# Attention outputs kept transposed, divided per chunk of queries on GpSimd, in a fused attention and mixture-of-experts kernel

## The chip, the cores and the metric

The kernel runs on one core of one Trainium2 chip. The metric is device time in microseconds (us). Before the change the median of three runs is 1865.36 us (1862.76 to 1872.71). All durations and starts below come from one further, profiled execution.

## The reference

One pre-layer-norm transformer block on x of 2048 tokens by 512 features, in float32:

```
Q = norm(x) @ Wq + bq          # 32 heads of 16
K, V = norm(x) @ Wk + bk, norm(x) @ Wv + bv    # 8 heads of 16, each shared by 4 query heads
out = softmax(Q K^T / 4) V     # per head, all 2048 keys
x = x + out @ Wo + bo
logits = norm(x) @ gate_w.T    # 8 experts
w, idx = softmax over the two largest logits, their experts
x = x + sum of w * (norm(x) @ expert_w[idx].T + expert_b[idx])
```

## The kernel before

The engines run streams that were written by hand, each in program order, joined by semaphores. There are 16 token tiles of 128 (`NKT`), 4 chunks of 512 queries (`NC`), 8 groups of heads (`G`), each of 4 query heads with one key head (`REP`), and so 32 rounds (`N`), one for each group and chunk.

**Rounds.** Each round has 16 steps (`kt`, one key tile of 128). A step (`attention_step`) puts on TensorE two `max_unit` (L722: scores of a later round, 128 queries by 1024 keys, that VectorE reduces to maxima, L1040), four score units (L751: keys on the partitions, 512 queries on the columns), and the value products of the step two before (L761). ScalarE takes the exponential of each score unit (L591). The value product has 32 output rows for each head: 16 of the value and 16 equal rows with the sum of the exponentials, for 512 queries on the columns. So the outputs come out transposed, in bank 6, and ScalarE copies them to `o_acc` (L581).

**The ring of banks.** Score units go round three PSUM banks (`SBANKS`). The list `RING` holds the order of what takes a bank. Besides the 64 score units of a round it holds `outputs` (before score unit 16, step 4) and `maxima` (before score unit 44, step 11). `ring_bank_free` makes each entry wait for whatever used the entry three places before. Entry `outputs` is four transposes of `o_acc` (`output_transpose`, L775). VectorE divides them by the sums (`normalise`, L1064 and L1066) into `o_norm`, which is stored in `heads_out` with queries on the partitions. Entry `maxima` is one transpose of the 16 columns of maxima (L732). From it VectorE makes the two rows that shift the scores of the next round (`make_shift`, L1054 and L1057), right behind one more reduction (L1040) in its program.

**Output stage.** After the last round, for each of 16 token tiles, TensorE transposes the loaded heads (L866), ScalarE rounds them to the high part (L597) and VectorE makes the low part (L1112). TensorE multiplies with Wo, split in the same way, in 12 matmuls (L856). VectorE adds the residual (L1147, after GpSimd added the bias `bo` to it, L369) and takes mean and variance (L1153, L1150). The tiles of the chunk before are in the same loop: normalised on VectorE (L1120), transposed on TensorE (L873), copied by ScalarE to `xgT` (`gate_evac`, L608), multiplied with the gate weights (`gate_logits`, L883). The square root of the variance is taken once for each chunk of four tiles (L627). Four times 128 logits are copied (L613) and turned back (L893). The stage ends when VectorE gets the last of them (`gl_full`). In it the expert weights of four of eight experts are split (`expert_hi` L599, `expert_lo` L1107); the others come after it.

**After it.** A chain of small operations on VectorE chooses experts and slots, indirect DMAs of GpSimd scatter the tokens, 39 slots of 128 tokens go through the experts, and the results are gathered and summed. The change touches the last two stages only in where the splits of three or four experts stand.

Of the kernel before, what the change touches and what calls it, by code (L numbers as in the profile page):

```python
# [16 lines left out]
def preln_attention_moe(nc, x, Wq, bq, Wk, bk, Wv, bv, Wo, bo, gate_w, expert_w, expert_b, out):  # L17
# [39 lines left out]
    RING.insert(REP * 4, ("outputs", 0))  # L57
    RING.insert(REP * (MAX_T + 1) + 1, ("maxima", 0))
# [16 lines left out]
    heads_out = nc.dram_tensor("heads_out", [NC, P, TT, G + 1, REP * DK], F32).ap()  # L75
# [4 lines left out]
    with ExitStack() as ctx:  # L80
# [23 lines left out]
        mv = sb("mv", [P, TT, 2])  # L104
        std = sb("std", [P, TT])
# [10 lines left out]
        o_rec = sb("o_rec", [P, TT, REP, 1])  # L116
        o_norm = sb("o_norm", [P, TT, REP, DK])
# [16 lines left out]
        with nc.sbuf_tensor("we_raw", [P, E, KD, D], F32) as we_raw:  # L134
# [35 lines left out]
        EA = 4  # L170
        (_, xg, xgT, lgT, _, atT_hi, atT_lo, at), (we_hi, x2T_hi, x2T_lo) = in_turn(
            [("we_hi_early", [P, EA, KD, D], F32R),
             ("xg", [P, 2, D], F32), ("xgT", [P, 2, KD, P], F32),
             ("lgT", [E, CH], F32),
             ("spare", [P, 3 * D], F32),
             ("atT_hi", [P, 2, KD, P], F32R), ("atT_lo", [P, 2, KD, P], F32R),
             ("at", [P, 2, TT, D], F32)],
            [("we_hi", [P, E, KD, D], F32R), ("x2T_hi", [P, 2, KD, P], F32R), ("x2T_lo", [P, 2, KD, P], F32R)])

# [47 lines left out]
        oT_full = sem("oT_full")  # L227
        rec_ready = sem("rec_ready")
        onorm_ready = sem("onorm_ready")
        o_dma = sem("o_dma")  # L230
        at_dma = sem("at_dma")
        xr_dma = sem("xr_dma")
# [5 lines left out]
        at_full = sem("at_full")  # L238
        at_hi = sem("at_hi")
        at_evac = sem("at_evac")  # L240
        wo_full = sem("wo_full")
        x2_ready = sem("x2_ready")
        step_c = sem("step_c")
        mv2_ready = sem("mv2_ready")
# [42 lines left out]
        B_OUT, B_MAX = ring_bank(("outputs", 0)), ring_bank(("maxima", 0))  # L287
# [4 lines left out]
        def _(pool):  # L292
# [70 lines left out]
            pool.wait_ge(s_full, UNITS * N)  # L363
            for c in range(NC):
                pool.dma_start(x2_all[:, c * TT:(c + 1) * TT, :], x_t[:, c * TT:(c + 1) * TT, :]).then_inc(xr_dma, 16)
                pool.wait_ge(xr_dma, 16 * (c + 1))
# [22 lines left out]
        def _(sp):  # L389
# [49 lines left out]
            def store_heads(i):  # L439
                wait_first(onorm_ready, 1 + i + 1)  # L440
# [81 lines left out]
        def _(act):  # L522
# [92 lines left out]
            def chunk(c, with_gate, last):  # L615

                for t in range(TT):
                    if not (last and t == TT - 1):
                        attention_hi(TT * c + t + 1, t + 1)
# [679 lines left out]
```

## Time and profile before

| | us |
|---|---|
| median of 3 runs | 1865.36 |
| profiled execution, its own time | 1858.62 |
| its span | 1857.0 |
| first round begins | about 152 |
| `o_acc` of the last round copied (L581) | 1514.85 |
| last logits turned back (L893) | 1606.91 |
| first scatter (L375) | 1620.89 |
| last expert matmul ends, about | 1801.7 |

TensorE is busy for 1692.8 us (91% of the span), VectorE for 1449.9 us (78%), ScalarE for 1251.2 us (67%), GpSimd for 162.9 us (9%). Busy shares say which engine is loaded. Which wait ends last in a stretch must be read from the rows of that stretch.

### The profile page before, as it was taken

Reading aid. Unit: us, or ns where it says so; the run is one execution under the profiler, and the core shown is the slowest. Engines: PE = TensorE matmul, PEld = TensorE weight load, DVE = VectorE, ACT = ScalarE, POOL = GpSimd, SP = SyncE. Lnnn points to the kernel's source line nnn. Section 1 sums busy time; section 2 is a strip of 40 time slices with the busy share of each in tenths; the row PEclk is TensorE's granted clock in tenths of the full one; section 3 lists DMA queues with packets and bytes.
Section 4 is the critical chain, followed back from the end, with each engine's and each line's share of the span. In section 5 each row is a group of like instructions: output and inputs, shape, how many; then the busy total and the mean of one; then the engine's idle time right before and its main releaser. Section 6 shows DMA issues by size and latency. Waiting matters only on the chain.

```text
span 1857.0 us, 38115 instructions
## 1 busy us (share of the span) xinstructions
PE 1692.8 (91%) x13946; PEld 814.3 (44%) x13947; DVE 1449.9 (78%) x1503; ACT 1251.2 (67%) x2291; POOL 162.9 (9%) x186
## 2 busy tenths in 40 slices
PE   6899999999999999999999999999999998569980
PEld 3533444444444444444444444444444456427860
DVE  3298999999999999999999999999999426552215
ACT  2325888888788888888888888888888863403320
POOL 3111110000000000000000000000000013070006
PEclk9998999999999999999999999999999999869995
DMA  6337332311211131113111111111120022044548
GB/s 198 83 108 162 111 110 67 70 30 22 57 29 22 22 61 22 22 22 64 34 24 44 24 22 22 44 22 22 22 44 27 5 97 69 12 170 154 167 135 256
DMA packets 76537, 125.15 MB, mean 67 GB/s; under 512 B 27976, under 2 KB 31576, under 8 KB 75648
## 3 DMA queue, kind: packets, MB, share of 16 engines
q1 hardware_dynamic: 61664, 80.38, 18.5%
q0 software_dynamic: 12304, 41.07, 6.6%
q10 hardware_dynamic: 2448, 1.84, 0.6%
q8 instruction: 106, 1.74, 0.4%
q14 instruction: 15, 0.12, 0.0%
HBM read 74.22 MB, written 47.84 MB: 66 GB/s over the span
## 4 chain that ended last, share of the span: by engine, by line
PE 82%; issue 6%; DVE 4%; POOL 3%; DMA 2%; ACT 1%; ACTq 0%; SPq 0%; DVEq 0%; POOLq 0%
PE bank L761 30%; PE bank L722 22%; PE bank L751 14%; PE bank L856 8%; PE bank L694 3%; POOL slots_x L375 1%; PE bank L775 1%; PE bank L932 1%; POOL ys L384 1%; POOL xs L384 1%; DVE o_norm L1066 1%; DVE max_kc L1040 1%; PE bank L883 1%; PE bank L709 1%; DMA arena_p<-in_L_attn_bv 1%
## 5 line engine op out<-in xcount | busy, mean ns | idle before, releaser
L1040 DVE TENSOR_REDUCE max_kc<-bank 128x1 f32<-128x1024 f32 x1024 | 1241.9, 1223 | 104.0 <-PE bank L722 84.2
L591 ACT ACTIVATE arena_p<-bank 128x512 f32<-128x512 f32 x2048 | 1108.2, 596 | 235.9 <-PE bank L751 205.0
L761 PE MATMUL bank<-arena_p,v_cur 128*32 128x256 f32 x8192 | 655.4, 392 | 3.2 <-issue 0.3
L722 PE MATMUL bank<-k_st,q_st 48*128 48x512 f32 x2048 | 513.6, 499 | 5.3 <-DMA q_st<-q_parts 4.0
L751 PE MATMUL bank<-q_st,k_st 50*128 50x512 f32 x2048 | 443.7, 411 | 33.6 <-DVE o_norm L1066 21.8
L722 PEld LDWEIGHTS bank<-k_st,q_st 48*128 48x128 f32 x2048 | 191.2, 184 | 422.4 <-issue 372.6
L751 PEld LDWEIGHTS bank<-q_st,k_st 50*128 50x128 f32 x2048 | 286.2, 185 | 80.1 <-DVE o_norm L1066 32.0
L761 PEld LDWEIGHTS bank<-arena_p,v_cur 128*32 128x32 f32 x8192 | 162.7, 108 | 292.7 <-issue 159.7
L1179 DVE TENSOR_TENSOR x2T_lo<-bank,x2T_hi 128x512 fp32r<-128x512 f32 x39 | 27.0, 691 | 103.9 <-ACT x2T_hi L597 103.9
L326 POOL COPY v_cur<-v_all 128x256 f32 (+1 forms) x8 | 3.2, 399 | 1054.7 <-PE bank L761 1054.7
L694 PE MATMUL bank<-xT,arena_p 128*128 128x512 f32 x160 | 83.7, 648 | 5.0 <-DMA arena_p<-in_L_attn_bv 2.9
L651 ACT ACTIVATE ys<-bank 128x512 f32<-128x512 f32 x39 | 23.3, 597 | 84.2 <-PE bank L856 84.2
L551 ACT ACTIVATE qf<-bank,bq_sb 128x512 f32<-128x512 f32 x16 | 11.0, 687 | 66.2 <-PE bank L694 66.2
L856 PE MATMUL bank<-we_hi,x2T_hi 128*128 x156 | 46.5, 420 | 0.1
L1064 DVE RECIPROCAL o_rec<-bank 128x16 f32<-128x16 f32 x33 | 8.2, 249 | 48.1 <-PE bank L775 48.1
L694 PEld LDWEIGHTS bank<-xT,arena_p 128*128 128x128 f32 x160 | 28.6, 199 | 35.6 <-issue 29.6
L375 POOL DMA_INDIRECT slots_x<-xn,slot_i x32 | 37.3, 1165 | 71.7 <-DVE slot_i L1222 61.1
L856 PE MATMUL bank<-we_hi,x2T_lo 128*128 x156 | 42.6, 395 | 0.0
L856 PE MATMUL bank<-we_lo,x2T_hi 128*128 x156 | 42.0, 391 | 0.0
L1268 DVE SCALAR_TENSOR_TENSOR x_all<-xs,g_w,x_all 128x512 f32<-128x512 f32 x16 | 12.1, 754 | 31.9 <-DMA ys<-slots_y,slot_i 31.9
L335 POOL TENSOR_TENSOR parts<-qf,parts 128x512 fp32r<-128x512 f32 x20 | 25.4, 1268 | 117.7 <-ACT parts L553 117.7
L608 ACT ACTIVATE xgT<-bank 128x512 f32<-128x512 f32 x16 | 9.6, 597 | 36.5 <-PE bank L873 36.5
(147 smaller groups left out, 811.5 us busy)
## 6 DMA issues: line engine op xcount, KB each, us to landing
q_st<-q_parts SPq DMA_DIRECT2D x192, 128.0 KB, 4.9
slots_x<-be_sb POOLq DMA_DIRECT2D x39, 256.0 KB, 2.3
xs<-slots_x SPq DMA_DIRECT2D x39, 256.0 KB, 2.7
slots_y<-ys SPq DMA_DIRECT2D x39, 256.0 KB, 2.0
q_parts<-parts SPq DMA_DIRECT2D x16, 512.0 KB, 3.0
we_raw<-in_L_ffn_expert_w POOLq DMA_DIRECT2D x8, 1024.0 KB, 6.4
k_st<-k_parts SPq DMA_DIRECT2D x48, 128.0 KB, 5.1
heads_out<-o_norm SPq DMA_DIRECT2D x33, 128.0 KB, 2.3
```

The lines of the kernel that those rows point to most:

```text
L335: pool.tensor_tensor(parts[:, u, 1, :], qf[:, u, :], parts[:, u, 0, :].bitcast(F32), ALU.subtract).then_inc(parts_ready, 1)
L375: pool.indirect_dma_start(slots_x, bass.IndirectOffsetOnAxis(ap=slot_i[:, a, n:n + 1], axis=0), xn2[:, n % SR, :], None).then_inc(sc_dma[n ...
L384: pool.indirect_dma_start(buf[:, n % SR, :], None, slots_y, bass.IndirectOffsetOnAxis(ap=slot_i[:, a, n:n + 1], axis=0)).then_inc(yt_dma[n ...
L591: act.activation(probs[:, u % PRING, :], bank[:, ring_bank(("score", u)), :], ACT.Exp, scale=SCALE).then_inc(p_ready, 1)
L651: act.activation(ys[:, b, :], bank[:, b, :], ACT.Copy).then_inc(y_evac, 1)
L694: mm = pe.matmul(bank[:, PROJ_BANK[p], :], w, xT[:, c, k, :], start=(k == 0), stop=(k == KD - 1))
L722: return pe.matmul(bank[:, 2 + 2 * (m % 2) + q, :], q_st[r:r + CROW, j % SLOTS, h, qt * P:(qt + 1) * P], k_st[r:r + CROW, j // NC % KSLOTS ...
L751: pe.matmul(bank[:, ring_bank(("score", u)), :], k_st[r:r + ROWS, i // NC % KSLOTS, kt * P:(kt + 1) * P], q_st[r:r + ROWS, i % SLOTS, h, : ...
L761: mm = pe.matmul(bank[32 * h:32 * h + 32, 6, half], v_cur[:, kt, :], probs[:, (REP * kt + h) % PRING, half], start=(kt == 0 and part == 0) ...
L856: mm = pe.matmul(out_, a(k), w(k), start=(q == 0 and k == 0), stop=(q == 2 and k == KD - 1))
L1040: dve.reduce_max(max_kc[:, m:m + 1], bank[:, 2 + 2 * (m % 2):4 + 2 * (m % 2), :].rearrange("p a s -> p (a s)"), AX.X).then_inc(m_done, 1)
L1179: dve.tensor_tensor(x2T_lo[:, b, :, :], bank[:, 5 + b, :].rearrange("p (k s) -> p k s", k=KD), x2T_hi[:, b, :, :], ALU.subtract).then_inc( ...
```

## The change

**Rounds.** The entry `outputs` is gone, with the four transposes, the division and their wait. `o_acc` is stored as it is (`store_heads`: 128 rows of 512 queries). Without `outputs` the ring would have 65 entries, which three banks don't divide. So an entry `none` is put behind `maxima`: a place that nobody uses. `ring_bank_free` goes three places further back from it.

**Division.** For each chunk of queries SyncE loads the 32 rows of sums back from DRAM (`load_sums`), VectorE takes their reciprocals (128 x 128, `reciprocal_sums`), and SyncE stores these and loads them again, spread over 16 partitions for each head (`rec_b`), beside the outputs (`at_n`), in eight DMAs of 256 KB. GpSimd multiplies (128 x 2048) and rounds the high part (128 x 2048). VectorE makes the low part (`attention_lo`, 128 x 2048). There is one buffer `at_n`, so a chunk is loaded only after the low part of the one before is made. Chunks 0 and 1 can be loaded during the last rounds.

**Output stage.** No transposes of heads. The Wo product of tile n goes to one of four banks (`2 + n % 4`, before: one of two). Variance, square root and normalisation go tile by tile instead of chunk by chunk. The gate transposes run three tiles behind the product, the gate logits four. Residual loads wait for the scores of one round each instead of for all. Five experts instead of four are split before the end of the stage.

```diff
-    RING.insert(REP * 4, ("outputs", 0))
-    RING.insert(REP * (MAX_T + 1) + 1, ("maxima", 0))
+    RING[REP * (MAX_T + 1):REP * (MAX_T + 1)] = [("maxima", 0), ("none", 0)]
...
                 r = RING.index(entry) - len(SBANKS)
+                if RING[r][0] == "none":
+                    r -= len(SBANKS)
...
-                elif kind == "outputs":
-                    pe.wait_ge(onorm_ready, 2 + i)
                 else:
                     pe.wait_ge(neg_ready, min(i, N - 2) + 3)
...
-                if kt == BEHIND + 1:
-                    output_transpose(i)
...
+            def residual(c):
+                pool.wait_ge(s_full, UNITS * (N - NC + c + 1))
+                pool.dma_start(x2_all[:, c * TT:(c + 1) * TT, :], x_t[:, c * TT:(c + 1) * TT, :]).then_inc(xr_dma, 16)
...
+            def normalise_attention(c):
+                pool.wait_ge(at_dma, 16 * 2 * KD * (c + 1))
+                pool.tensor_tensor(at_n[:, :, :], at_n[:, :, :], rec_b[:, :, :], ALU.mult).then_inc(at_norm, 1)
+            def attention_hi(c):
+                pool.wait_ge(at_norm, c + 1)
+                if c == 1:
+                    pool.wait_ge(pv_done, PRING // REP + NKT * N)
+                if c >= 2:
+                    pool.wait_ge(wo_full, TT * (c - 1))
+                pool.tensor_copy(at_hl[c % 2][:, 0, :, :], at_n[:, :, :]).then_inc(at_hi, 1)
+            residual(0)
+            add_bias_o(0)
+            normalise_attention(0)
+            attention_hi(0)
+            residual(1)
+            add_bias_o(1)
+            normalise_attention(1)
+            residual(2)
+            add_bias_o(2)
+            residual(3)
+            attention_hi(1)
+            normalise_attention(2)
+            add_bias_o(3)
+            for c in range(2, NC):
+                if c > 2:
+                    normalise_attention(c)
+                attention_hi(c)
...
+            def load_attention(c):
+                sp.wait_ge(rec_ready, c + 1)
+                sp.dma_start(sums_rec[c].rearrange("f (a q) -> f a q", q=P), sums[:, c % 2, :]).then_inc(rec_dma, 16)
+                if c == 0:
+                    sp.wait_ge(v_ready, G)
+                else:
+                    sp.wait_ge(at_lo, c)
...
```

The loops of the output stage, of ScalarE, of TensorE and of VectorE in this order (`deviation2` waits for the variance, `gate_logits` for `gate_evac`, `residual_add` for the product):

```diff
+            for n in range(NKT + 4):
+                if 1 <= n <= NKT:
+                    deviation2(n - 1)
+                if n >= 4:
+                    gate_evac(n - 4)
...
+            for n in range(NKT + 3):
+                if n < NKT:
+                    attention_tile(n)
+                if n >= 4:
+                    gate_logits(n - 4)
+                if n >= 3:
+                    gate_transpose(n - 3)
...
+            reciprocal_sums(NC - 1)
+            attention_lo(1)
+            for n in range(NKT + 2):
+                if n < NKT:
+                    residual_add(n)
+                if 1 <= n <= NKT:
+                    variance(n - 1)
+                if n < NKT:
+                    statistics(n)
+                if n >= 2:
+                    gate_tile(n - 2)
+                if n == TT or n == 2 * TT:
+                    attention_lo(n // TT + 1)
+                if n == 3 or n == 7:
+                    expert_lo(n // 4)
+                if n >= NKT - 1:
+                    expert_lo(2 + n - (NKT - 1))
```

How the change moves instructions, at three places. In the program after the change the lines are numbered anew.

TensorE before, one regular round, steps 10 and 11 around the transpose of the maxima (L732); L722 are the maximum units, L751 the score units, L761 the value products:

```order
L761 MATMUL bank<-arena_p,v_cur 32x256 x4
L732 MATMUL bank<-ident,max_q 16x128 [waits maxq_ready,p_ready]
L722 MATMUL bank<-k_st,q_st 128x512 [waits m_done]
L722 MATMUL bank<-k_st,q_st 128x512
L751 MATMUL bank<-q_st,k_st 128x512 [waits p_ready] x2
L761 MATMUL bank<-arena_p,v_cur 32x256 [waits p_ready]
L761 MATMUL bank<-arena_p,v_cur 32x256 x3
L722 MATMUL bank<-k_st,q_st 128x512 [waits m_done]
L722 MATMUL bank<-k_st,q_st 128x512
L751 MATMUL bank<-q_st,k_st 128x512 [waits neg_ready]
L751 MATMUL bank<-q_st,k_st 128x512 [waits p_ready]
L761 MATMUL bank<-arena_p,v_cur 32x256 x4
```

TensorE after, the same place (L774 the transpose, L764 maximum units, L793 score units, L803 value products):

```order
L803 MATMUL bank<-arena_p,v_cur 32x256 x4
L774 MATMUL bank<-ident,max_q 16x128 [waits maxq_ready,p_ready]
L764 MATMUL bank<-k_st,q_st 128x512 [waits m_done]
L764 MATMUL bank<-k_st,q_st 128x512
L793 MATMUL bank<-q_st,k_st 128x512 [waits p_ready]
L793 MATMUL bank<-q_st,k_st 128x512 [waits neg_ready]
L803 MATMUL bank<-arena_p,v_cur 32x256 [waits p_ready]
L803 MATMUL bank<-arena_p,v_cur 32x256 x3
L764 MATMUL bank<-k_st,q_st 128x512 [waits m_done]
L764 MATMUL bank<-k_st,q_st 128x512
L793 MATMUL bank<-q_st,k_st 128x512 [waits p_ready] x2
L803 MATMUL bank<-arena_p,v_cur 32x256 x4
```

The wait for the shift rows (`neg_ready`) was at score unit 46, behind four value products and a maximum unit. Now it is at score unit 45, ahead of them.

ScalarE before, two tiles of the output stage (L597 the high part of the heads, L608 the copy to `xgT`, L627 the square root of a chunk):

```order
L597 ACTIVATE atT_hi<-bank 128x512 [waits at_full]
L608 ACTIVATE xgT<-bank 128x512 [waits gt_full]
L627 ACTIVATE std<-mv,eps_sb 128x4 [waits mv2_ready]
L597 ACTIVATE atT_hi<-bank 128x512 [waits at_full]
L608 ACTIVATE xgT<-bank 128x512 [waits gt_full]
```

ScalarE after, three tiles of the output stage (L663 the square root of one tile, L654 the copy to `xgT`):

```order
L663 ACTIVATE std<-mv,eps_sb 128x1 [waits var_ready]
L654 ACTIVATE xgT<-bank 128x512 [waits gt_full]
L663 ACTIVATE std<-mv,eps_sb 128x1 [waits var_ready]
L654 ACTIVATE xgT<-bank 128x512 [waits gt_full]
L663 ACTIVATE std<-mv,eps_sb 128x1 [waits var_ready]
L654 ACTIVATE xgT<-bank 128x512 [waits gt_full]
```

A square root, which waits for VectorE's variance, now stands ahead of every copy to `xgT`.

VectorE after, one tile of the output stage (L1134 the residual, L1147 the variance, L1142 the statistics, L1151 and L1156 the normalisation of an earlier tile):

```order
L1134 TENSOR_TENSOR x_all<-bank,x_all 128x512 [waits xb_ready,wo_full]
L1147 BN_AGGR mv<-stats 128x2 [waits stats_ready]
L1142 BN_STATS stats<-x_all 128x6 [waits x2_ready,var_ready]
L1151 RECIPROCAL rstd<-std 128x1 [waits std2_ready]
L1156 TENSOR_SCALAR xg<-x_all,mv,rstd 128x512 [waits rstd_ready,gt_evac]
```

The variance of the tile before stands behind the residual addition, which waits for TensorE's product of this tile (`wo_full`).

## Rows read from the trace of the kernel before

**Rows 1.** Page, part 4: the chain that ended last, shares of the span by engine.

```profile
PE 82%; issue 6%; DVE 4%; POOL 3%; DMA 2%; ACT 1%; ACTq 0%; SPq 0%; DVEq 0%; POOLq 0%
```

**Rows 2.** Line 326 alone: GpSimd's step once in four rounds; ns, first and last start.

```profile
L326 POOLq FUSED_REGOPS  x7: 58/58/58, 330.8 to 1355.2; - x7
```

**Rows 3.** Timeline, undisturbed steps of a round: start, length, engine, line, operation [idle before <-releaser].

```profile
828.48 16.18 DVE L1040 TENSOR_REDUCE max_kc<-bank 128x1 f32<-128x1024 f32 x13 [0.47 <-PE bank L722]
```

**Rows 4.** Timeline, TensorE around the transposes of the outputs.

```profile
846.89 0.50 PE L722 MATMUL bank<-k_st,q_st 48*128 48x512 f32 x2
...
848.13 0.66 PE L775 MATMUL bank<-ident,o_acc 128*128 128x128 f32 x4
...
851.16 0.50 PE L751 MATMUL bank<-q_st,k_st 50*128 50x512 f32 x2 [0.71 <-DVE o_norm L1066]
...
852.16 0.50 PE L722 MATMUL bank<-k_st,q_st 48*128 48x512 f32 x2
```

**Rows 5.** Timeline, TensorE and VectorE around the transpose of the maxima.

```profile
867.64 0.59 PE L751 MATMUL bank<-q_st,k_st 50*128 50x512 f32 x2
867.84 1.22 DVE L1040 TENSOR_REDUCE max_kc<-bank 128x1 f32<-128x1024 f32 x1 [0.23 <-PE bank L722]
...
869.62 0.51 PE L751 MATMUL bank<-q_st,k_st 50*128 50x512 f32 x2 [0.39 <-DVE shift L1057]
870.05 0.64 PE L761 MATMUL bank<-arena_p,v_cur 128*32 128x256 f32 x8
...
870.62 0.50 PE L722 MATMUL bank<-k_st,q_st 48*128 48x512 f32 x2
```

**Rows 6.** Timeline, end of the last round and first Wo product.

```profile
1514.85 0.60 ACT L581 ACTIVATE o_acc<-bank 128x512 f32<-128x512 f32 x1 [1.45 <-PE bank L761]
...
1519.39 1.20 PE L856 MATMUL bank<-wo_hi,atT_hi 128*128 128x512 f32 x4 [1.05 <-DVE atT_lo L1112]
```

**Rows 7.** Timeline, output stage, one tile.

```profile
1582.27 1.17 PE L856 MATMUL bank<-wo_hi,atT_hi 128*128 128x512 f32 x4
...
1585.64 1.04 PE L883 MATMUL bank<-xgT,wg_sb 128*8 128x128 f32 x8
...
1586.62 0.66 PE L866 MATMUL bank<-ident,at 128*128 128x128 f32 x4
1587.03 1.17 PE L856 MATMUL bank<-wo_hi,atT_hi 128*128 128x512 f32 x4
...
1590.07 0.69 DVE L1147 TENSOR_TENSOR x_all<-bank,x_all 128x512 f32<-128x512 f32 x1 [0.26 <-PE bank L856]
...
1590.68 0.17 DVE L1150 BATCH_NORM_AGGREGATE mv<-stats 128x2 f32<-128x6 f32 x1
```

**Rows 8.** Timeline, ScalarE: square root of a chunk, next activation.

```profile
1577.83 0.30 ACT L627 ACTIVATE std<-mv,eps_sb 128x4 f32<-128x4 f32 x1 [1.49 <-DVEq L1161]
...
1578.03 0.58 ACT L597 ACTIVATE atT_hi<-bank 128x512 fp32r<-128x512 f32 x1
```

**Rows 9.** Timeline, TensorE: last step of the output stage.

```profile
1606.91 0.41 PE L893 MATMUL bank<-ident,lgT 8*128 8x8 f32 x4 [0.68 <-ACT lgT L613]
```

**Rows 10.** Groups by line and shape: xcount | busy us, mean ns | idle before.

```profile
L335 POOL TENSOR_TENSOR parts<-qf,parts 128x512 fp32r<-128x512 f32 x20 | 25.4, 1268 | 117.7 <-ACT parts L553 117.7
L1107 DVE TENSOR_TENSOR we_lo<-we_raw,we_hi 128x2048 fp32r<-128x2048 f32 x6 | 13.9, 2313 | 0.0
L326 POOL COPY v_cur<-v_all 128x256 f32 x7 | 2.8, 400 | 1054.7 <-PE bank L761 1054.7
```

**Rows 11.** DMA issues: xcount, KB each, median us to landing.

```profile
heads_out<-o_norm SPq DMA_DIRECT2D x33, 128.0 KB, 2.3
at<-heads_out SPq DMA_DIRECT2D x4, 1024.0 KB, 6.6
```

**Rows 12.** Stretches: us, busy us of each engine (instructions), granted clock, DMA share, GB/s.

```profile
1540.00:1543.00 3.00, 3.00 (x13) 2.73 (x13) 1.60 (x4) 1.19 (x2) 0.80 (x1) 0.56 0.44 180
1641.00:1650.00 9.00, 7.54 (x13) 2.62 (x12) 6.56 (x13) 1.11 (x4) 7.48 (x6) 0.62 0.43 164
```

More of the change, by code:

```diff
@@ L115, in preln_attention_moe @@
         o_acc = sb("o_acc", [P, CH])
-        o_rec = sb("o_rec", [P, TT, REP, 1])
-        o_norm = sb("o_norm", [P, TT, REP, DK])
+        sums = sb("sums", [P, 2, P])
+        lgT = sb("lgT", [E, CH])
         gates = sb("gates", [P, NKT, E])
@@ L459, in _ @@
                 load_keys(g, kr_dma)
-            for i in range(N - 2):
-                store_heads(i)
-                place_shift(i + 1)
+            for i in range(N):
+                if i > 0:
+                    store_heads(i)
+                if i > N - NC:
+                    load_sums(i - (N - NC) - 1)
+                if i < N - 1:
+                    place_shift(i + 1)
                 if i + SLOTS < N:
@@ L654, in _ @@
             act.activation(g_exp[:, 1, :, :], g_exp[:, 0, :, :], ACT.Exp).then_inc(ge_ready, 1)
-            for e in range(EA, E):
+            act.wait_ge(wo_full, NKT)
+            for e in ORDER[EA:]:
                 expert_hi(e)
@@ L766, in value_product @@
                     mm.then_inc(pv_done, 1)
-            def output_transpose(i):
-                pe.wait_ge(o_ready, i + 1)
-                if i == N:
-                    pe.wait_ge(p_ready, len(SBANKS) + UNITS * N)
-                else:
-                    ring_bank_free(i, ("outputs", 0))
-                for t in range(TT):
-                    mm = pe.transpose(bank[:, B_OUT, t * P:(t + 1) * P], o_acc[:, t * P:(t + 1) * P], ident[:, :])
-                mm.then_inc(oT_full, 1)
             steps = [(p, k) for p in range(EARLY, len(PROJ)) for k in range(KD)]
@@ L859, in _ @@
             pe.wait_ge(m_done, 2 + MUNITS * N)
-            pe.wait_ge(o_ready, N + 1)
             pe.wait_ge(p_ready, len(SBANKS) + UNITS * N)
             pe.wait_ge(wlo_ready, 1)
-            def transpose_attention(n, t, half):
-                pe.wait_ge(at_evac, n + 1)
-                for k in range(KD):
-                    mm = pe.transpose(bank[:, 2 + t % 2, k * P:(k + 1) * P], at[:, half, t, k * P:(k + 1) * P], ident[:, :])
-                mm.then_inc(at_full, 1)
             def gate_transpose(g):
@@ L1084, in round_ @@
                             reduce_unit(j, m + half)
-                        if kt == 4 and half == 0:
-                            normalise(i)
+                        if kt == 4 and half == 0 and i_is(N - 2):
+                            reciprocal_sums(0)
                         if kt == MAX_T + 1 and half == 0 and not last:
```

279 lines of the change are left out of this document (114 added, 165 removed).

## Prediction, made before the changed kernel ran

> **What bounds the kernel now.** I read the chain that ended last first: TensorE holds 82% of it [rows 1]. So I looked at what paces TensorE in each stretch. GpSimd passes one place of its program once in four rounds, seven times: (1355.2 - 330.8) / 24 = 42.68 us a round [rows 2]. Sixteen undisturbed steps would be shorter: 13 reductions in 16.18 us make 1.245 us for half a step, 39.8 us for 32 [rows 3]. The rest, 2.85 us, is lost at two known places. Around the output transposes the maximum units (L722) start at 846.89 and, three half steps on, at 852.16: 5.27 us where 3.73 would do. That is 1.53 us lost, in four transposes (started 848.13) and in score unit 16, which waits for `o_norm` [rows 4]. Around the transpose of the maxima the reduction of 867.84 must end before VectorE makes the shift rows. TensorE goes on at 869.62, and the next maximum unit starts at 870.62 [rows 5]. The third place is the output stage. From the end of the last value product (I call it E, 1514.8, where ScalarE begins to copy `o_acc`) it takes 4.6 us to the first Wo product [rows 6]. The last logits are back at 1607.3, E + 92.5 [rows 9]. A tile takes 4.76 us there: 1582.27 to 1587.03 [rows 7].
>
> **The change, part by part.**
>
> *Outputs leave the ring.* In 31 rounds 1.53 us goes [rows 4], also in round 0. The last round has no maximum units and is paced by the exponentials, so I take half, 0.7. Sum -48. VectorE's 0.7 us of division vanishes in that wait. `o_acc` is stored from DRAM row to row. SyncE has over 30 us for it before the next copy, so I count nothing. What is late next at this place is only TensorE itself, at its own 1.245 us.
>
> *The wait for the shift moves.* Before, score unit 44 and 45 went ahead (867.64), then four value products and a maximum unit, and only score unit 46 waited until 869.62 [rows 5]. After, unit 45 waits for the same shift rows. VectorE makes them at the same time as before, for they stand behind the reduction of 867.84, which is not moved. Behind unit 45 on TensorE are four value products, a maximum unit, and two score units. So at 869.62 unit 45 starts, and from there everything comes that before had come during the wait. Value products at 869.95 to 870.05, maximum unit 0.57 later, and the next maximum unit one half step (1.245) after it, at 871.8 instead of 870.62. That is +1.15 us, with bounds of 0.5 (if VectorE catches up) and 1.25 (a whole half step). Unit 44 now waits for the exponential just before it, which ends at about 867.7, so nothing. 30 rounds make +34.5, round 30 (which has no reduction ahead of the shift) +0.3. Sum +35. The rounds together: -13, between -33 and -10.
>
> *Start of the output stage.* Chunk 0 can be ready before E, since VectorE, GpSimd and SyncE are idle for most of the last round. So the first product starts at E + 0.1 instead of E + 4.6 [rows 6]. Tiles 0 to 3 have four banks and need nothing more: a product and four transposes are 3.37 us [rows 7], the transposes 0.41, so 2.9 for a product, E + 11.5 for four. VectorE is late for them: the last sums go out (copy 0.6, store 2.3), come back (2.3) [rows 11], are inverted (0.5, not in the trace; between 0.2 and 1.2 by the 0.25 us that 16 columns take, estimate), and then the low part of chunk 1 is made, 2.3 us by the 128 x 2048 subtraction [rows 10]. That is E + 8.5. The first gate tile is normalised three residual steps later, at E + 14, and its transposes wait for it 2.5 us.
>
> *Chunk 2.* SyncE may load it when that low part is made, at E + 8.6. Two megabytes in eight DMAs, where one megabyte takes 6.6 [rows 11]: 9 us (7 to 13), E + 17.5. GpSimd multiplies: four times the 1.27 us of 512 columns [rows 10], 5.1. Then, in program order, the four bias additions of chunk 3, 5.1, E + 27.7. Then the high part: by the copy of 256 columns at 0.40 us [rows 10] 3.2 at most; I take 2.8, bounds 2 and 5. E + 30.5. VectorE's low part ends at E + 32.8. It stands in VectorE's program behind tile 4, so the residual of tile 5 waits for it, and behind that its variance, ScalarE's square root, `xgT`, and TensorE's logits. TensorE has finished the product of tile 5 at about E + 24.5, and goes on at E + 34.6. Ten microseconds of idle TensorE. It then starts at the lower clock: after the 3.3 us wait before 1539.7 the granted clock of 1540 to 1543 was 0.56 [rows 12], at a cost of some 1.5 us. So tile 6 begins at E + 37.5.
>
> The Trainium skill, page "GPSIMD Engine Reference", section "Engine selection", advises VectorE for elementwise work, since two-input operations are about twice as slow on GpSimd and one-input ones nearly at line rate; section 3 has 4.50 us for a two-input 128 x 2048 against 2.29. The rows agree (5.1 and 2.3). By its figures the multiplication, the additions and the rounding would end some 2 us earlier, and the total would be 2 us lower.
>
> *The pace of the stage.* Now I follow one tile, from the start of its product. VectorE adds the residual 3.1 us after (1587.03 to 1590.07), and takes a variance 0.61 after that, 0.17 long [rows 7]: 3.9. ScalarE's square root follows, and the next activation starts 0.20 behind it and takes 0.58 [rows 8]: 4.75. Only this activation, the copy to `xgT`, releases the gate logits that stand behind the product on TensorE. Its own input was ready a whole tile earlier. It waits in ScalarE's program behind the square root, that in VectorE's behind the residual of this tile. Then logits 0.98 and transposes 0.41 [rows 7]: 6.15 us a tile, in which TensorE idles 1.85. Before it was 4.76, with four transposes more. Tiles 6 to 15: 61.5. The copy of 512 logits stands in the way twice, 0.6 each, and four turns 0.4 each: +2. E + 101.
>
> *The end of the stage.* Three low parts of experts (2.3 each [rows 10]) now stand between VectorE's last gate tiles, where nothing else hides them. By the same steps (logits 12 to 15, transposes 13 to 15, each behind a copy to `xgT`, and 4.6 us of experts) it takes 12 us: E + 113. Before: E + 92.5. The stage is +20.5 before any further loss of clock, and I add 3 for that. One expert less is split after the stage, where it is hidden, nothing.
>
> **The sum.** -13 + 20.5 + 3 = +10.5, against the profiled execution's own time: 1858.6 + 10.5 = 1869. That execution is 6.7 below the median of the three runs shown, so on the scale of the medians 1865.4 + 10.5, which I round to 1875.
>
> **The rivals.**
> - *The stage is not slower.* If the copies to `xgT` don't wait for this tile's variance, TensorE's own 4.3 us decide (2.9 + 0.98 + 0.41), and the stage ends between E + 83 and E + 92, with the wait for chunk 2 inside. The total breaks even at about 5.1 us a tile (23.5 - 13 = 10.5 over ten tiles less than 6.15); below it the change gains. Total 1843 to 1855. For it: four banks, and a stage of few instructions. Against it: the order on three engines is fixed.
> - *The wait at the shift costs no more than before.* Then the rounds keep their -48, and with the stage's +23.5 the total is 1841. For it: VectorE can reduce faster than TensorE feeds it. Against it: the reduction ahead of the shift ends when it ends [rows 5].
> - *Lower clock through the stage.* With an idle 1.85 us in each 6.15, the clock may fall between tiles: in 1641 to 1650 it was 0.62 with TensorE busy 7.54 of 9 us [rows 12]. If it is at 1.2 GHz for a third of the stage, 4.3 us of work becomes 8.6 in every third tile and hides part of the wait: +10 to +15, total 1888. The Trainium skill speaks for it: "TensorE: Matmul & The Clock Gate", section "A second HAM failure mode: psum-queue depth-cycling", has a kernel whose short idles between groups of matmuls made the clock swing between its levels.
> - *It cancels out.* GpSimd and the DMAs at their lower bounds (6 us less) and the clock untouched: 1866.
>
> **How the numbers follow.** Forecast as worked out 0.47, cancels out 0.20, lower clock 0.18, stage not slower 0.10, shift for free 0.05. A measurement of this kernel can tell 0.5%, 9.3 us, from no change. Slower by more: most of the lower clock and 0.32 of the forecast's 0.47, 0.50. Within: 0.37. Faster by more: 0.13. The range of 8 in 10 is 1857 to 1891; that of the likeliest case alone 1867 to 1884.
>
> **What would show it.** A round of 42.3 us instead of 42.68. Score units with about 1.6 us of idle before them, released by VectorE's shift, and no wait on any output division. First product within 0.3 us of E. A gap of about 10 us on TensorE near E + 25, with VectorE waiting for GpSimd's rounding. Starts of products 6.1 us apart from tile 6 on, logits released by the copy to `xgT`, and that behind the square root. The stage's end at E + 113. If products are under 5 us apart, my chain through ScalarE is wrong; if the round is under 41.5, my account of the shift is.

## The result: 9% slower, and where 180 us went

The changed kernel takes 2040.22 us (median of 4 runs, 2026.41 to 2071.55), against 1865.42 for the kernel before (its median with one run more than above). The ratio is 1.091 (95% interval 1.084 to 1.097; ratios leave out disturbed runs, which are the longest run here and the longest of e2). I had forecast 1875 and a range of 1857 to 1891. The sign was right, the size was wrong by far. The profiled execution took 2038.73 us, 180 more than that of before. Here are, from the pages, the TensorE clock in tenths for 40 slices of the span, before:

```profile
PEclk9998999999999999999999999999999999869995
```

and changed, with the chain that ended last, which answers to [rows 1]:

```profile
PEclk9895989899699897978789969989899987967995
...
PE 82%; issue 5%; POOL 4%; DMA 3%; DVE 3%; ACT 1%; SPq 1%; ACTq 1%; POOLq 0%; DVEq 0%
```

The chain has hardly moved. It names TensorE for 82%, as before. What is new is the clock row. The whole of the rounds is one row in each kernel (from, to, length, busy us of PE, PEld, DVE, ACT and POOL with their instructions, granted clock, DMA share, GB/s). First before, then changed:

```profile
153.00:1515.00 1362.00, 1324.84 (x12351) 575.68 (x12348) 1224.76 (x1136) 1123.88 (x2081) 33.62 (x59) 1.00 0.19 42
```

```profile
156.00:1654.00 1498.00, 1452.96 (x12228) 589.11 (x12225) 1216.03 (x1076) 1128.48 (x2081) 54.28 (x71) 0.88 0.19 45
```

The granted clock has two levels, so a mean of 0.88 means that 24% of 1498 us, some 360 us, ran at 1.2 GHz. The reader sees TensorE busy for 128 us more with 123 instructions fewer: that is nearly the same work, part of it at half the clock, and not a wait. The rounds start 3.6 us later (first copy of `o_acc` at 159.92 for 156.31) and end (the last copy of `o_acc`, which answers to the first row of [rows 6]) at 1654.03 instead of 1514.85. That is 139 of the 180 us. The output stage takes 136 us instead of 92.5, 43.6 more. What follows it is 2.8 us shorter.

Where does the clock fall? This is the place of [rows 5] in the changed kernel, in a round in which it falls. The timeline, TensorE and VectorE, has start, length, engine, line, operation, and the idle time before with its releaser:

```profile
852.55 0.49 PE L764 MATMUL bank<-k_st,q_st 48*128 48x512 f32 x2
852.99 0.50 PE L793 MATMUL bank<-q_st,k_st 50*128 50x512 f32 x1
853.08 1.23 DVE L1053 TENSOR_REDUCE max_kc<-bank 128x1 f32<-128x1024 f32 x1 [0.23 <-PE bank L764]
854.22 0.27 DVE L1067 TENSOR_SCALAR shift<-bank 16x128 fp32r<-16x128 f32 x1
854.53 0.28 DVE L1070 SCALAR_TENSOR_TENSOR shift<-bank,shift 16x128 fp32r<-16x128 f32 x1
...
854.86 0.49 PE L793 MATMUL bank<-q_st,k_st 50*128 50x512 f32 x1 [1.37 <-DVE shift L1070]
855.28 0.64 PE L803 MATMUL bank<-arena_p,v_cur 128*32 128x256 f32 x8
855.85 0.68 PE L764 MATMUL bank<-k_st,q_st 48*128 48x512 f32 x2
...
856.57 1.22 DVE L1053 TENSOR_REDUCE max_kc<-bank 128x1 f32<-128x1024 f32 x1 [1.77 <-PE bank L764]
...
858.74 1.23 DVE L1053 TENSOR_REDUCE max_kc<-bank 128x1 f32<-128x1024 f32 x1 [0.94 <-PE bank L764]
860.90 1.22 DVE L1053 TENSOR_REDUCE max_kc<-bank 128x1 f32<-128x1024 f32 x1 [0.94 <-PE bank L764]
```

Score unit 45 waits 1.37 us for the shift rows, where unit 46 had waited 0.39. From 856 on the reductions (one for each half step) start 2.16 us apart, not 1.245, and each is released by the maximum unit: TensorE paces them at half the clock. The stretch that follows, as a window:

```profile
856.10:890.10 34.00, 34.00 (x192) 10.84 (x190) 19.49 (x16) 17.58 (x33) 0.00 (x0) 0.50 0.16 32
```

So one wait of 1.37 us is followed by 34 us at 1.2 GHz. It is not so in every round. From the second round on there are 29 such waits, each of 1.37 us. Behind 19 of them the clock fell, for 3.4 to 34.1 us, and behind ten it stayed up. The falls begin between 0.1 us before the end of the wait and 2.0 us behind it. From one copy of `o_acc` to the next, seven rounds (the fourth and sixth among them) stay at 2.4 GHz throughout and take 42.34 to 42.41 us, which is what I forecast for all. The others, up to the thirtieth, take 44.8 to 55.0, the first 61.5.

The first round needs a word of its own. Its low stretch begins at 159.7 us, ahead of the first of these waits (at 201), and is 47.8 us long. Such a first stretch is in every kernel: 10.2 us before, and below 27.3 in e1, 10.2 in e5 and 37.5 in e2, where it is over before the first long wait. So the 15 us that the first round lost (61.5 for 46.6) can't be put down to the wait. What makes the first stretch long or short wasn't tried.

### The profile page after: what moved, and what is told of

Same layout as the page of the kernel before. It is cut to its first block, busy times and chain, and to the rows that moved or that the text cites. A ratio compares the mean times of both kernels' runs of the same rounds, so it can differ in the third digit from the quotient of the medians.

```text
span 2037.1 us, 37579 instructions
## 1 busy us (share of the span) xinstructions
PE 1823.8 (90%) x13750; PEld 826.3 (41%) x13751; DVE 1441.8 (71%) x1437; ACT 1248.3 (61%) x2287; POOL 184.7 (9%) x194
## 4 chain that ended last, share of the span: by engine, by line
PE 82%; issue 5%; POOL 4%; DMA 3%; DVE 3%; ACT 1%; SPq 1%; ACTq 1%; POOLq 0%; DVEq 0%
PE bank L803 31%; PE bank L764 24%; PE bank L793 14%; PE bank L884 7%; PE bank L736 3%; POOL slots_x L417 1%; DMA rec_b<-sums_rec 1%; PE bank L945 1%; POOL xs L426 1%; PE bank L906 1%; POOL ys L426 1%; POOL at_n L385 1%; DVE max_kc L1053 1%; PE bank L751 1%; PE bank L896 0%
## 5 line engine op out<-in xcount | busy, mean ns | idle before, releaser
L803 PE MATMUL bank<-arena_p,v_cur 128*32 128x256 f32 x8192 | 727.0, 430 | 2.8 <-issue 0.3
L764 PE MATMUL bank<-k_st,q_st 48*128 48x512 f32 x2048 | 559.5, 544 | 4.9 <-DMA q_st<-q_parts 3.7
L793 PE MATMUL bank<-q_st,k_st 50*128 50x512 f32 x2048 | 486.4, 444 | 42.1 <-DVE shift L1070 41.2
L764 PEld LDWEIGHTS bank<-k_st,q_st 48*128 48x128 f32 x2048 | 207.0, 199 | 496.3 <-issue 329.3
L793 PEld LDWEIGHTS bank<-q_st,k_st 50*128 50x128 f32 x2048 | 300.0, 208 | 82.8 <-DVE shift L1070 51.4
L803 PEld LDWEIGHTS bank<-arena_p,v_cur 128*32 128x32 f32 x8192 | 169.3, 113 | 353.6 <-issue 233.4
L906 PE MATMUL bank<-xgT,wg_sb 128*8 128x128 f32 x128 | 20.6, 316 | 39.1 <-ACT xgT L654 28.3
L663 ACT ACTIVATE std<-mv,eps_sb 128x1 f32<-128x1 f32 x16 | 4.7, 293 | 81.4 <-DVE mv L1147 81.4
L736 PEld LDWEIGHTS bank<-xT,arena_p 128*128 128x128 f32 x160 | 28.3, 198 | 33.3 <-issue 28.3
L1088 DVE TENSOR_TENSOR at_hl<-at_n,at_hl 128x2048 fp32r<-128x2048 f32 x4 | 9.2, 2290 | 43.3 <-POOL at_hl L393 43.3
L1134 DVE TENSOR_TENSOR x_all<-bank,x_all 128x512 f32<-128x512 f32 x16 | 11.0, 686 | 39.6 <-PE bank L884 39.6
```

The costliest lines, as they stand in the source:

```text
L736: mm = pe.matmul(bank[:, PROJ_BANK[p], :], w, xT[:, c, k, :], start=(k == 0), stop=(k == KD - 1))
L764: return pe.matmul(bank[:, 2 + 2 * (m % 2) + q, :], q_st[r:r + CROW, j % SLOTS, h, qt * P:(qt + 1) * P], k_st[r:r + CROW, j // NC % KSLOTS ...
L793: pe.matmul(bank[:, ring_bank(("score", u)), :], k_st[r:r + ROWS, i // NC % KSLOTS, kt * P:(kt + 1) * P], q_st[r:r + ROWS, i % SLOTS, h, : ...
L803: mm = pe.matmul(bank[32 * h:32 * h + 32, 6, half], v_cur[:, kt, :], probs[:, (REP * kt + h) % PRING, half], start=(kt == 0 and part == 0) ...
L906: mm = pe.matmul(bank[0:E, 6, t * P:(t + 1) * P], wg_sb[:, d, :], xgT[:, g % 2, d, :], start=(d == 0), stop=(d == KD - 1))
```

## The experiments

All ratios are to the kernel before on the same chip, which took 1868 to 1870 us. Where a run is compared with the changed kernel, which was timed beside 1865.42, some 4 us of the difference may be that. Theory A: the longer wait at unit 45 makes the granted clock fall, and this is most of the 139 us. Rivals: something else in the change lowers the clock (B), or the new stage is the main loss (C).

**The unused place ahead of the maxima (e1_none_ahead).**

```diff
-    RING[REP * (MAX_T + 1):REP * (MAX_T + 1)] = [("maxima", 0), ("none", 0)]
+    RING[REP * (MAX_T + 1):REP * (MAX_T + 1)] = [("none", 0), ("maxima", 0)]
```

> The changed kernel with the unused place in the ring ahead of the maxima instead of behind, so score unit 45 goes ahead again and only unit 46 waits for the shift rows. Theory A (the longer wait at unit 45 makes the granted clock fall): the rounds stay at full clock, a round takes 41.1 to 41.2 us (42.68 less 1.53), the last outputs are copied near 1470 and not 1654, total 1835 to 1860 us. Theory B (something else in the change lowers the clock: the missing transposes, the stores, bank order): the granted clock still falls to 0.5 in the rounds, total over 1980. Theory C (the new output stage is the main loss): total falls by the 35 us of the wait alone, about 2005.

Measured: 1853.64 us (1847.53 to 1863.64), ratio to before 0.992 (0.988 to 0.996). The regular round takes 41.3 us. The rounds as one row:

```profile
155.00:1481.00 1326.00, 1302.66 (x12221) 565.32 (x12221) 1213.11 (x1076) 1124.43 (x2081) 56.23 (x72) 0.99 0.22 50
```

A round is 0.1 us over what I expected, and the last copy of `o_acc` comes at 1481.55, not near 1470. Some 6 of these 11 us are the first round (52.8 us for 46.6), which has its 27.3 us of low clock. From 186 us on the clock is at its upper level to the end of the rounds. Unit 46 now waits for the shift, and in the list of who waited for the shift rows (200 to 1440 us; us, times) the waits are short:

```profile
  PE bank L793: 15.6, 29
```

That is 0.54 us each. In the changed kernel the same list, with the same line number, has 1.37:

```profile
  PE bank L793: 37.0, 27
```

Two entries of the list swapped give back 187 us. B and C fall: everything else of the change is still in this kernel. The new stage costs its 39 us here too (131.9 for 92.5), but it is not the main loss.

**The wait alone, put into the kernel before (e2_before_unit45_waits).**

```diff
                 ring_bank_free(i, ("score", u))
+                if u == REP * (MAX_T + 1) + 1:
+                    pe.wait_ge(neg_ready, min(i, N - 2) + 3)
```

> The kernel before, with one wait more: score unit 45 also waits for the shift rows. Theory A: the granted clock falls in many rounds behind that wait, as in the changed kernel: 30 to 35 us of wait and some 150 us at the lower clock, total 1990 to 2060. Theory B: only the wait itself, 1.15 us in 30 rounds, total 1885 to 1900, clock 1.0 in the rounds.

Measured: 2138.7 us (2127.15 to 2192.43), ratio 1.141 (1.134 to 1.148): 270 us for one wait. It went further than A expected. Here the clock falls behind all 30 of these waits, for 10 to 41 us, and from the seventh round to the thirtieth each takes 51.2 us. The rounds, and the list of waits for the shift rows:

```profile
154.00:1796.00 1642.00, 1564.68 (x12367) 614.86 (x12367) 1228.89 (x1138) 1128.81 (x2083) 33.85 (x59) 0.83 0.16 35
```

```profile
  PE bank L753: 40.3, 24
```

A wait is 1.68 us here, and the wait for the division of the outputs is there as well. The other parts of the change are not needed for the effect. Whether the wait for the division, which the changed kernel doesn't have, adds to it here wasn't tried.

**Work put into the wait (e5_filled_wait).** The changed kernel, with seven matmuls ahead of unit 45 whose results nobody reads (in front of them stands the wait for the exponential that frees their bank):

```diff
...
+                for x in range(7):
+                    pe.matmul(bank[:, ring_bank(("none", 0)), :], k_st[r:r + ROWS, i // NC % KSLOTS, 0:P],
+                              q_st[r:r + ROWS, i % SLOTS, 0, :], start=True, stop=True)
```

> The changed kernel, with seven matmuls of 50x128 by 50x512 added ahead of score unit 45, written to the bank of the unused place and read by nobody (1.5 us of TensorE work inside the wait for the shift rows). Theory A: the clock stays at 1.0 in the rounds, a round takes 42.3 to 42.6 us although it has more work, total about 1880 to 1895, some 150 us below the changed kernel. Theory B: the added work does nothing for the clock, total 2030 to 2080.

Measured: 1885.07 us (1879.79 to 1889.64), ratio 1.009 (1.005 to 1.012). TensorE has 32 times 1.5 us more to do, and the kernel is 155 us faster. Every regular round takes 42.31 to 42.34. The rounds:

```profile
153.00:1506.00 1353.00, 1348.76 (x12452) 605.32 (x12448) 1215.81 (x1076) 1127.98 (x2081) 56.30 (x72) 1.00 0.21 50
```

Unit 45 starts behind the same event as before, so the time of the wait is unchanged and only TensorE's idleness in it is gone. This separates "it waits" from "it is idle", and it is idleness that costs. It also shows that my figure for a round, 42.3 us, was right at the clock for which I made it. All rounds together take 9 us less than before, where I had 13: 0.36 us less in each regular round, nothing less in the first, and 1 us more in the last, which has the added matmuls but no such wait.

**The shift rows made earlier (e11_after_shift_first; e10_before_shift_first).** VectorE makes them ahead of the reduction that had stood before them, in the changed kernel and in the kernel before:

```diff
+                        if kt == MAX_T + 1 and half == 0 and not last:
+                            make_shift(i + 1, 0)
+                            make_shift(i + 1, 1)
                         if not isinstance(i, int) or j < N:
                             reduce_unit(j, m + half)
-                        if kt == MAX_T + 1 and half == 0 and not last:
-                            make_shift(i + 1, 0)
-                            make_shift(i + 1, 1)
```

> The changed kernel (unused place behind the maxima) with the shift rows ahead of the reduction. The wait at score unit 45 begins and ends earlier, at most 0.6 us instead of 1.4. Theory A (the clock falls with the length of this wait): the rounds stay at full clock, a round about 41.0 to 41.4 us, total 1845 to 1870. Theory B (a wait at unit 45 lowers the clock whatever its length): the clock still falls in many rounds, total over 1950.

Measured: 1843.1 us (1838.18 to 1847.91), ratio 0.986 (0.983 to 0.989). Both the round (40.9 us) and the total are a little under my range. Unit 45 still stands behind the shift rows, but in the list of waits no matmul of L793 stands any more, only weight loads with 0.23 us each:

```profile
  PEld bank L793: 7.0, 30
```

The clock is 1.00 from 200 to 1440 us. With the wait at the same place and shorter, the clock stays up.

> The kernel before, with nothing changed but the place of the shift rows in VectorE's program: ahead of the reduction. If this saving has nothing to do with the outputs in the ring: a round 41.8 to 41.9 us instead of 42.68, total 22 to 28 us below before, 1837 to 1846. If the division of the outputs in VectorE's program hides it: within 8 us of before.

Measured: 1848.73 us (1843.26 to 1851.42), ratio 0.990 (0.988 to 0.992). The round takes 42.02 us. The gain of 19.5 us is under what I expected: I had taken 0.85 us a round, it is 0.66.

**ScalarE's order in the stage (e3_evac_first).** In e1, the copy to `xgT` ahead of the square root:

```diff
-                if 1 <= n <= NKT:
-                    deviation2(n - 1)
                 if n >= 4:
                     gate_evac(n - 4)
+                if 1 <= n <= NKT:
+                    deviation2(n - 1)
```

> The kernel of e1 with, in ScalarE's loop of the output stage, the copy to xgT ahead of the square root of the newer tile. If my chain through ScalarE sets the pace: products 4.4 to 4.8 us apart where nothing else disturbs (6.1 in the changed kernel), the stage 12 to 18 us shorter, total 12 to 20 us below e1. If the pace is set by VectorE or by the bank: pitch stays about 6.1 and the total within 4 us of e1.

Measured: 1833.87 us (1826.6 to 1838.77), ratio 0.979 (0.975 to 0.984), 20 below e1. Products start 4.31 us apart in undisturbed tiles, a little under the 4.4 to 4.8 that I expected. Every fourth tile takes 1.5 to 2 us more, since the copy of the logits still stands behind a square root. The stage takes 116.2 us instead of 131.9. In e1 the undisturbed pitch is 6.06, as in the changed kernel, and only this order differs. So the chain through ScalarE sets it.

**GpSimd's order (e4_gpsimd_order).** In e3:

```diff
-            residual(0)
-            add_bias_o(0)
+            for c in range(3):
+                residual(c)
+                add_bias_o(c)
             normalise_attention(0)
             attention_hi(0)
-            residual(1)
-            add_bias_o(1)
             normalise_attention(1)
-            residual(2)
-            add_bias_o(2)
             residual(3)
             attention_hi(1)
-            normalise_attention(2)
             add_bias_o(3)
             for c in range(2, NC):
-                if c > 2:
-                    normalise_attention(c)
+                normalise_attention(c)
```

VectorE makes the reciprocals of chunk 3 behind its third tile and not ahead of the low part of chunk 1, and the low parts of chunks 2 and 3 two tiles later.

> The kernel of e3 with another order on GpSimd and VectorE in the output stage: GpSimd adds the bias to the residuals of chunks 0 to 2 before the first multiplication, rounds chunk 1 right behind its multiplication, and adds the bias to chunk 3 ahead of the multiplication of chunk 2; VectorE makes the low part of chunk 1 ahead of the reciprocals of chunk 3 and the low parts of chunks 2 and 3 two tiles later. Theory A (the two long stalls of TensorE, 11 and 12 us, come from what stands ahead of the roundings in GpSimd's program): both shrink to under 4 us together, stage 15 to 20 us shorter than in e3 (116 us), total 1810 to 1822. Rival (the loads of 2 MB for a chunk set the time): the stage is under 6 us shorter, total 1828 to 1835.

Measured: 1823.01 us (1819.89 to 1824.72), ratio 0.976 (0.970 to 0.982), 11 below e3 and 1 us over my range. In the profile the stage is 98.3 us, 18 shorter, so the rival falls. How much of it is GpSimd's order and how much VectorE's, which was changed with it, this run doesn't divide. The first gate transposes start 15.4 us after the end of the rounds, behind 4.37 us of idle TensorE instead of 11.44, and the second long stall is gone. The two waits of TensorE for a gate tile that are left are together 5.6 us, not under 4:

```profile
1492.32 1.11 PE L891 MATMUL bank<-ident,xg 128*128 128x128 f32 x4 [4.37 <-DVE xg L1151]
...
1504.82 0.66 PE L891 MATMUL bank<-ident,xg 128*128 128x128 f32 x4 [1.21 <-DVE xg L1151]
```

**Smaller steps and the best version.** In e6_early_reciprocals (e4 with this edit, for which SyncE's `load_attention` is divided in two) the loads of `rec_b` no longer stand behind those of `at_n`, and wait only for the multiplication of the chunk before:

```diff
...
-                    sp.wait_ge(at_lo, c)
+                    sp.wait_ge(at_norm, c)
...
```

> The kernel of e4 with the spread reciprocals of a chunk loaded as soon as GpSimd has multiplied the chunk before, and only the outputs after its low part is made. If the load is on the path: 1 MB less behind each low part, some 5 us earlier for chunks 2 and 3, total 3 to 8 us below e4. If not: within 3 us of e4.

Measured: 1821.37 us (1810.78 to 1828.31), ratio 0.975 (0.968 to 0.983). The profile has 5 us less in the stage (93), the medians of four runs don't tell it from e4. Inconclusive.

e7_shift_first is e6 with the diff of e11:

> The kernel of e6 with VectorE making the shift rows ahead of the reduction that stood before them, not behind it. VectorE is free when the maxima are transposed, so unit 46 hardly waits: a round takes 40.2 to 40.6 us instead of 41.3, total 25 to 33 us below e6. Rival (the delayed reduction holds up the next maximum unit instead): the round stays within 0.3 us of 41.3, total within 8 us of e6.

Measured: 1790.8 us (1787.38 to 1796.81), ratio 0.959 (0.953 to 0.966), 30.6 below e6. The round takes 40.49 us. No rival wait appears: TensorE is busy 1287.83 of 1295 us in the rounds.

e8_stage_tail is e6 with the end of the stage changed (one expert fewer is split in it):

```diff
-                if n >= NKT - 1:
-                    expert_lo(2 + n - (NKT - 1))
...
+            expert_lo(2)
...
+                if n >= 8 and n % TT == 0:
+                    logits_evac(n // TT - 2)
                 if 1 <= n <= NKT:
                     deviation2(n - 1)
...
```

> The kernel of e6 with the low parts of three experts taken from between the last gate tiles (one behind them, one behind the scatter, one expert left to the later loop) and the copy of the logits ahead of the square root. VectorE's 6.9 us at the end of the stage go and tiles 8 and 12 lose their extra 1.5 us: total 5 to 10 us below e6. Rival: the gate tiles wait for the copies to xgT anyway, total within 3 us of e6.

Measured: 1809.46 us (1808.12 to 1810.81), ratio 0.969 (0.963 to 0.975), 12 below e6, a little more than expected.

e9_both is e7 and e8 together:

> The kernel of e7 (shift rows first) with the end of the stage as in e8. If the two savings lie on one path and add: 12 us below e7, total 1775 to 1785. If the start of the stage or the lower clock behind it takes it back: 1785 to 1795.

Measured: 1785.41 us (1781.24 to 1791.74), ratio 0.956 (0.953 to 0.958): 4.4% faster than the kernel before and 12.5% faster than the changed one. The stage is 83.3 us, 12 shorter than in e7, as expected. Of the median only 5 arrives, which is the second case of what I expected. In the profiles the first round takes 2.8 us longer than in e7, and the part behind the stage 2. What makes them longer wasn't tried. The row of its last logits answers to [rows 9]; the last copy of `o_acc` is at 1451.2:

```profile
1534.11 0.41 PE L916 MATMUL bank<-ident,lgT 8*128 8x8 f32 x4 [0.68 <-ACT lgT L662]
```

## Why the prediction was wrong, step by step

**Outputs leave the ring: right.** In e1 the round is 41.3 us instead of 42.68, 1.38 less for 1.53. The difference, 0.15, is that unit 46 now waits 0.54 us for the shift and not 0.39.

**The wait for the shift moves: near in its length (1.37 us of idle where I wrote about 1.6), wrong in its price. This is the step that failed.** I wrote that the next maximum unit comes "one half step (1.245) after it" and charged "+1.15 us, with bounds of 0.5 and 1.25". The seven undisturbed rounds and all of e5 confirm the wait itself. What it does to the granted clock I left out of the sum altogether. At 1.2 GHz half a step takes 2.16 us instead of 1.245, so 0.42 of the time there is lost. That is 148 us of the 350 that the changed kernel spends there beyond the 10 of before. Some 132 of them stand behind the waits, in the 19 stretches (310 us together), and 16 in the first round's own stretch, which begins ahead of the first wait. So the price of the wait is not 35 us but 35 + 132. With my -13 the 148 make 135, and the rounds grew by 135.6 (139.2 less the later start); that it comes out so closely is chance, for e5 has -9 and not -13. The upper bound of a wait that the trace before does not contain had to include this. A row from which to suspect it was there: [rows 12] had a clock of 0.56 after a wait. But I used it for the output stage alone, as a rival with 0.18, since in the rounds of before the clock never fell after the first.

The Trainium skill, "TensorE: Matmul & The Clock Gate", section "HAM oscillation — how this bites in real kernels", describes a clock that falls back in every pass of a loop, and puts it down to long waits for DMA. This case has the swing, in e2 in every round, with a wait of under 1.7 us on an engine that is busy for 95% of the time. Its next section, "A second HAM failure mode: psum-queue depth-cycling", which I had cited for the stage, comes nearer: there short idle times between groups of matmuls are enough. But it speaks of frequent ones. Here the frequent ones, of 0.39 to 0.71 us, did nothing, and one of 1.37 us in a round was enough.

**Start of the output stage: right for the first product, wrong behind it.** It starts 0.1 us before the last `o_acc` copy (E is 1654.03 here). I had the first gate tile normalised at E + 14 and its transposes wait 2.5 us for it. They waited 11.44 us, until E + 22.5:

```profile
1655.23 0.79 POOL L375 DMA_DIRECT2D x_all<-in_L_attn_x  x1
...
1661.22 5.01 POOL L381 TENSOR_TENSOR x_all<-x_all,bo_sb 128x512 f32<-128x512 f32 x4 [5.21 <-DMA x_all<-in_L_attn_x]
...
1666.94 1.90 POOL L393 CAST at_hl<-at_n 128x2048 fp32r<-128x2048 f32 x1
1668.88 2.29 DVE L1088 TENSOR_TENSOR at_hl<-at_n,at_hl 128x2048 fp32r<-128x2048 f32 x1 [6.59 <-POOL at_hl L393]
...
1676.51 1.11 PE L896 MATMUL bank<-ident,xg 128*128 128x128 f32 x4 [11.44 <-DVE xg L1156]
```

I had taken it, without saying so, that GpSimd is done with chunk 1 when the rounds end. It wasn't: it issued the residual load of chunk 2 at 1655.23, waited for it, added four biases, and only then rounded chunk 1. VectorE's low part, behind which the first residual stands, started at E + 14.9 and not at E + 6.2. That is 8.7 us late, and everything of chunk 2 behind it as well. What is queued ahead on GpSimd I had named for chunk 2 only. The row of 1668.88 names the rounding as what VectorE waited for, and e4, with another order, has 4.37 us of this wait instead of 11.44.

**Chunk 2: durations near, start late.** GpSimd's multiplication takes 4.57 us (I took 5.1), the four additions 4.91 (5.1), the rounding 1.88 (2.8), VectorE's low part 2.29 (2.3). The load takes 13.9 us (1671.2 to 1685.06), where I had 9, with bounds of 7 and 13. The residual load of chunk 3, issued at 1666.17, lies mostly ahead of it, so I had the load itself too short: 1 MB in 6.6 us [rows 11] doesn't carry over to rows of 2 KB in eight DMAs. In e9 the 1 MB of outputs alone took 9.5 and 9.3 us. Whether the short rows or the number of DMAs makes it slower wasn't tried. TensorE's gap is 11.66 us where I said 10, and tile 6 starts at E + 48.8 instead of E + 37.5:

```profile
1700.22 1.87 PE L906 MATMUL bank<-xgT,wg_sb 128*8 128x128 f32 x8 [11.66 <-ACT xgT L654]
```

**The pace of the stage: right where nothing disturbs.** Two products from tile 6 on start 6.05 and 6.09 us after the one before, for 6.15. The others take 6.6 to 11.3; low parts, copies of logits and stretches at the lower clock stand among them. One tile, which answers to [rows 7]:

```profile
1747.39 2.09 PE L884 MATMUL bank<-wo_hi,at_hl 128*128 128x512 f32 x8
...
1750.44 0.69 DVE L1134 TENSOR_TENSOR x_all<-bank,x_all 128x512 f32<-128x512 f32 x1 [3.56 <-PE bank L884]
1751.04 0.17 DVE L1147 BATCH_NORM_AGGREGATE mv<-stats 128x2 f32<-128x6 f32 x1
1751.25 0.29 ACT L663 ACTIVATE std<-mv,eps_sb 128x1 f32<-128x1 f32 x1 [5.29 <-DVE mv L1147]
...
1751.45 0.58 ACT L654 ACTIVATE xgT<-bank 128x512 f32<-128x512 f32 x1
```

Product, residual, variance, square root, copy, in the order that I had worked out. e3 breaks this chain and the pitch is 4.31, the figure of my rival (4.3). I gave that rival a tenth, and in the changed kernel its condition did not hold: it needed an edit.

**The end of the stage.** E + 136 and not E + 113. Of the 23 us too few, 11 are there when tile 6 starts. Nine come between tiles 6 and 15 (65.4 us for 56.5). Five of them are one tile of 11.33 us, in which VectorE's operations stand still while GpSimd works (below); a copy of logits and 6.8 us of the lower clock fall into it too. The rest is at the end, partly at 1.2 GHz.

**The clock in the stage: too small.** I added 3 us, and for the wait near chunk 2 another 1.5. The mean clock of the stage is 0.82, for 0.98 before: 47.8 of the 136 us ran at 1.2 GHz, a third, which was the condition of my rival "lower clock through the stage". TensorE was busy in 28.3 of them. At 2.4 GHz that work would take about half, so the clock cost at most 14 us here. Part of it is in the late tiles named above and can't be added to them. The largest stretches (13.7 us each) lie around the two long waits.

## What to carry over

When an edit lengthens a wait of a nearly full TensorE, the price may be more than the wait. The trace of before, with its full clock in the rounds, did not say how near it was to falling (e2: one wait more, and it fell in every round); take as upper bound the stretch behind the wait at half the clock, and look for a way to shorten the wait or to put work into it. In a ring of banks, where an unused place stands decides which unit waits. And in front of every operation that the path needs, read the whole queue of its engine, the DMA waits that stand there for other data among it.

## What was not expected of the hardware

- Waits of 1.37 us, once in each round, on a TensorE busy for 97% of the time, were followed by up to 34 us at 1.2 GHz, and waits of 1.68 us (e2) always by 10 us or more. Behind waits of 0.39 and 0.54 us, and behind that for the division (0.71) [rows 4], it never fell after the first round. The summed idle time alone does not explain it: TensorE is idle for 37 of 1362 us of the rounds before and 45 of 1498 after, 2.7% and 3.0%. Before, it is in two short waits a round, after, in one long wait. The groups of score units on the two pages have theirs behind the second bar, 33.6 us before and 42.1 us after:

```profile
L751 PE MATMUL bank<-q_st,k_st 50*128 50x512 f32 x2048 | 443.7, 411 | 33.6 <-DVE o_norm L1066 21.8
```

```profile
L793 PE MATMUL bank<-q_st,k_st 50*128 50x512 f32 x2048 | 486.4, 444 | 42.1 <-DVE shift L1070 41.2
```

Why the clock falls behind 19 of the 29 waits of 1.37 us and not behind the other ten, and from what length on a wait is too long, the runs don't show.
- VectorE stood still beside GpSimd. The scaling of one tile took 3.90 us instead of 0.55, and the low part of an expert 3.97 instead of 2.28, in the changed kernel:

```profile
1714.34 4.57 POOL L385 TENSOR_TENSOR at_n<-at_n,rec_b 128x2048 f32<-128x2048 f32 x1 [18.00 <-DMA rec_b<-sums_rec]
1715.30 3.90 DVE L1156 TENSOR_SCALAR xg<-x_all,mv,rstd 128x512 f32<-128x512 f32 x1 [0.26 <-DVE rstd L1151]
...
1718.98 1.97 POOL L393 CAST at_hl<-at_n 128x2048 fp32r<-128x2048 f32 x1
1719.12 3.97 DVE L1127 TENSOR_TENSOR we_lo<-we_raw,we_hi 128x2048 fp32r<-128x2048 f32 x1
```

  Each ends within 0.3 us of GpSimd's end plus its own time: 1714.34 + 4.57 = 1718.91, and 0.55 makes 1719.46 for 1719.20. The Trainium skill, "SBUF — State Buffer", section "SBUF: two separate sides", describes such a lock: GpSimd and VectorE share a pair of ports, which one instruction holds to its end while the other engine is blocked. For VectorE it names instructions with two inputs in SBUF, beside a GpSimd instruction that reads SBUF, and those in a mode that uses both of its ports. The low part has two such inputs. The scaling has one, and no run shows in which mode it ran. The two rows agree with a lock. An operation moved to GpSimd to relieve VectorE stopped it here for up to 3.4 us.
